# Splitting the gather of a mixture-of-experts layer by halves of the experts

## The reference

```
affinity = softmax(x @ gate_w)                  # 512 tokens x 8 experts, per batch
gating, index = top_k(affinity.T, K=128)        # each expert picks its 128 tokens
x_sel = x[index]                                # 8 experts x 128 tokens x 128
h = silu(x_sel @ Wg[e]) * (x_sel @ Wu[e])       # 128 -> 256
out = (h @ Wd[e]) * gating                      # 256 -> 128
x_out = zeros.at[index].add(out)                # scatter back
```

## Time and profile before

| | before |
|---|---|
| median of three runs | 482.2 us |
| profiled execution, its time | 482.52 us |
| its span, first to last instruction | 480.8 us |
| TensorE busy | 397.7 us, 83% |
| VectorE busy | 385.2 us, 80% |
| ScalarE busy | 232.2 us, 48% |
| GpSimd busy | 54.5 us, 11% |
| mean granted TensorE clock | 0.933 |

### The profile page before, as it was taken

The page is one execution under the profiler, slowest core; times in us unless marked ns, Lnnn a source line. Parts: engine busy times, 40 slices in busy tenths (PEclk is TensorE's granted clock), DMA queues, the critical chain, the costliest instruction groups (busy, mean ns, idle before and its releaser), DMA issues.

```text
span 480.8 us, 7695 instructions
## 1 busy us (share of the span) xinstructions
PE 397.7 (83%) x2204; PEld 213.2 (44%) x2204; DVE 385.2 (80%) x841; ACT 232.2 (48%) x439; POOL 54.5 (11%) x103
## 2 busy tenths in 40 slices
PE   2702999999778889999999999999977019999995
PEld 1600456776543543333333333334427004567764
DVE  6698957788789888999898899987546889577883
ACT  2400453432341157777777777778863003543322
POOL 4520002122000010000000000000014400011210
PEclk9999999999897669999999999999996558999998
DMA  6100002223069721111112111100200000022103
GB/s 178 46 0 0 1 1 67 65 58 92 4 237 287 274 79 46 45 46 46 44 49 56 60 49 52 44 1 2 67 1 0 0 1 1 1 65 65 41 25 89
DMA packets 25767, 27.48 MB, mean 57 GB/s; under 512 B 3920, under 2 KB 17488, under 8 KB 25680
## 3 DMA queue, kind: packets, MB, share of 16 engines
q1 hardware_dynamic: 25744, 27.20, 18.6%
HBM read 17.08 MB, written 9.98 MB: 56 GB/s over the span
## 4 chain that ended last, share of the span: by engine, by line
PE 64%; DVE 16%; issue 12%; ACT 4%; POOL 1%; DMA 1%; DVEq 0%; ACTq 0%; POOLq 0%
PE ps L1151 14%; PE ps L1161 13%; PE ps L1136 6%; PE ps L1038 5%; DVE probs L748 4%; DVE neg_max L810 3%; PE ps L1021 3%; PE ps L1053 3%; PE ps L1023 3%; PE ps L1054 3%; PE ps L1022 3%; ACT probs L599 2%; PE ps L963 2%; PE ps L1170 2%; DVE heads_out L709 2%
## 5 line engine op out<-in xcount | busy, mean ns | idle before, releaser
L810 DVE TENSOR_REDUCE neg_max<-ps 128x1 f32<-128x512 f32 x256 | 161.1, 681 | 14.3 <-PE ps L1136 14.2
L599 ACT ACTIVATE probs<-ps 128x512 f32<-128x512 f32 x256 | 136.8, 601 | 44.0 <-PE ps L1151 42.8
L1136 PE MATMUL ps<-stacks 63*128 63x512 f32 x256 | 105.7, 494 | 3.3 <-DVE neg_max L810 2.6
L1151 PE MATMUL ps<-stacks 64*128 64x512 f32 x256 | 95.0, 462 | 4.9 <-ACT probs L599 4.8
L1151 PEld LDWEIGHTS ps<-stacks 64*128 64x128 f32 x256 | 41.3, 190 | 76.3 <-ACT probs L599 65.7
L1161 PE MATMUL ps<-probs,v_ext 128*32 128x512 f32 x512 | 69.0, 612 | 0.0
L1136 PEld LDWEIGHTS ps<-stacks 63*128 63x128 f32 x256 | 43.8, 196 | 19.5 <-DVE neg_max L810 15.0
L525 ACT CAST stacks<-ps 128x512 fp32r<-128x512 f32 x32 | 17.2, 588 | 67.5 <-PE ps L1002 67.5
L771 DVE TENSOR_TENSOR vae_and_gates<-heads_out,ps 128x512 f32<-128x512 f32 x32 | 21.9, 686 | 21.3 <-ACT heads_out L533 19.3
L453 POOL TENSOR_TENSOR w_lo<-w_gu,w_hi 128x512 fp32r<-128x512 f32 x16 | 20.6, 1295 | 150.1 <-ACT w_hi L512 150.1
L748 DVE TENSOR_TENSOR probs<-slot_row,slot 128x1024 f16<-128x1024 f16 x32 | 36.5, 1219 | 0.1
(11 more groups left out here) (150 smaller groups left out, 539.2 us busy)
## 6 DMA issues: line engine op xcount, KB each, us to landing
stacks<-parts_dram SPq DMA_DIRECT2D x64, 128.0 KB, 2.4
parts_dram<-part_hi SPq DMA_DIRECT2D x8, 512.0 KB, 3.5
parts_dram<-part_lo SPq DMA_DIRECT2D x8, 512.0 KB, 5.8
w_gu<-in_L_ffn_Wg_dram SPq DMA_DIRECT2D x16, 128.0 KB, 2.1
w_gu<-in_L_ffn_Wu_dram SPq DMA_DIRECT2D x16, 128.0 KB, 2.2
wd_sb<-in_L_ffn_Wd_dram SPq DMA_DIRECT2D x16, 128.0 KB, 2.2
x<-in_L_attn_x_dram SPq DMA_DIRECT2D x4, 256.0 KB, 3.7
stacks<-k_rows_dram SPq DMA_DIRECT2D x2, 512.0 KB, 6.6
```

Source lines behind the costliest of these rows:

```text
L599: nc.scalar.activation(probs[:, u // HG, u % HG, :], ps[:, RING + ring_bank(step, u), :], ACT.Exp, scale=SCORE_SCALE).then_inc(probs_ready, 1)
L810: nc.vector.tensor_reduce(neg_max[:, g, col, qt:qt + 1], ps[:, ring_bank(step, u), :], AX.X, ALU.max, negate=True).then_inc(max_taken, 1)
L1136: nc.tensor.matmul(ps[:, ring_bank(step, u), :], q_stack[rows, g, pp, chunk(qt)], k_stack[rows, g, pp, :], start=True, stop=True).then_inc ...
L1151: nc.tensor.matmul(ps[:, RING + ring_bank(step, u), :], k_stack[rows, g, pp, chunk(c)], q_stack[rows, g, pp, :], start=True, stop=True).th ...
```

## The change

The gather is divided by halves of the experts instead of by batches alone.

- VectorE makes the masks of experts 0 to 3 for all four batches first (16 instructions of 512 numbers per partition in place of 1024), and those of experts 4 to 7 in between the work for the first two experts.
- TensorE gathers experts 0 to 3 of all batches, starts `experts` when their 8 copies are done, and gathers the second half in four pieces: gate_up(0), gather, down(0), gather, gate_up(1), gather, gather. The four products of zeros that clear banks 0 to 3, and turn_down(0), come after these.
- ScalarE's copies of the second half, and the rounding of the weights of experts 2 and 3, stand in the new order too; the first turn of ScalarE's loop is written out.
- The facts are reduced in two halves, so that there are four reductions.
- Eight products of zeros into bank 2 (`WARM_UP`) come ahead of the gather.

```
-                for b in range(B):
-                    pe.wait_ge(halves_ready[l], b + 1)
-                    if b == 0:
-                        pe.wait_ge(facts_ready[l], CL)
-                    for hf in range(2):
...
+                for _ in range(WARM_UP):
+                    nc.tensor.matmul(ps[:, 2, :], zeros[:, 0:P], zeros[:], start=True, stop=True)
+                pe.wait_ge(facts_ready[l], CL)
+                for b in range(B):
+                    pe.wait_ge(halves_ready[l], b + 1)
+                    gather(l, b, 0)
+            def gather(l, b, hf):
+                if hf == 0 and b == 3:
+                    pe.wait_ge(picked_ready[l], 2)
+                if hf == 1:
+                    pe.wait_ge(picked_ready[l], 2 * B + 2 * max(b - 1, 0))
+                for c in range(C):
+                    pe.wait_ge(pick_ready[l], B * C * hf + C * b + c + 1)
+                    for bank, half in zip(pick_banks(b, hf), (xn_hi, xn_lo)):
+                        last = nc.tensor.matmul(ps[:, bank, :], half[:, C * b + c, :], pick[:, b, c, EH * hf:EH * hf + EH, :], ...)
+                last.then_inc(gathered[l], 1)
+                if hf == 1 and b == 0:
+                    pe.wait_ge(slot_facts_ready[l], 2)
+                for e in range(EH * hf, EH * hf + EH):
...
             def experts(l):
-                pe.wait_ge(picked_ready[l], 4 * B)
+                pe.wait_ge(picked_ready[l], 2 * B)
...
                 gate_up(0, 0)
-                pe.wait_ge(slot_facts_ready[l], 2)
+                gather(l, 0, 1)
+                down(0, 0)
+                gather(l, 1, 1)
+                gate_up(0, 1)
+                gather(l, 2, 1)
+                gather(l, 3, 1)
+                pe.wait_ge(slot_facts_ready[l], 4)
+                pe.wait_ge(picked_ready[l], 4 * B)
                 for b in range(B):
                     nc.tensor.matmul(ps[:, b, :], zeros[:, 0:P], zeros[:], start=True, stop=True)
-                down(0, 0)
-                gate_up(0, 1)
                 turn_down(0, 0)
```

VectorE's order in `experts` and ScalarE's:

```
+                make_picks(l, 0, 1)
+                read_facts(l, 0)
+                make_picks(l, 1, 1)
                 gate_times_up(0, 0)
                 dve.wait_ge(slot_facts_ready[l], 2)
                 make_place(0, 0)
+                make_picks(l, 2, 1)
                 gate_times_up(0, 1)
+                make_picks(l, 3, 1)
+                read_facts(l, 1)
                 weigh(0, 0, before=False)
...
                 silus(0, 0)
+                copy_picked(l, 0, 1)
+                copy_down(0, 0)
+                copy_picked(l, 1, 1)
+                silus(0, 1)
+                copy_picked(l, 2, 1)
+                copy_picked(l, 3, 1)
+                round_weights(l, 0, 2)
+                copy_down(0, 1)
+                silus(0, 2)
+                round_weights(l, 0, 3)
```

More of the change, by code:

```diff
@@ L275, in after, with pick_banks @@
             return i * (2 * per) + (per * o + more)
-        def pick_bank(n):
-            return 2 + 2 * (n % 3)
+        EH = E // 2
+        WARM_UP = 8
+        def pick_banks(b, hf):
+            if hf == 0:
+                return ((2, 3), (4, 5), (6, 7))[b % 3]
+            return ((2, 3), (0, 7))[b % 2]
         block = ctx.enter_context(nc.Block())
@@ L520, in route, with copy_picked @@
                 round_weights(l, 0, 1)
[L521 to L526, removed]
+                for b in range(B):
+                    copy_picked(l, b, 0)
+            def copy_picked(l, b, hf):
+                act.wait_ge(gathered[l], B * hf + b + 1)
+                for bank, picked in zip(pick_banks(b, hf), (picked_hi, picked_lo)):
+                    nc.scalar.copy(picked[:, EH * hf:EH * hf + EH, b, :],
+                                   ps[:, bank, :].rearrange("p (e s) -> p e s", e=EH)).then_inc(picked_ready[l], 1)
             def experts(l):
@@ L539, in experts @@
                 silus(0, 0)
-                with act.Fori(0, E // 2 - 1) as i:
+                copy_picked(l, 0, 1)
[8 more added lines that the diff above has]
+                round_weights(l, 0, 3)
+                with act.Fori(1, E // 2 - 1) as i:
                     for o in (1, 2):
@@ L746, in route, with make_picks, read_facts @@
                 for b in range(B):
[L747 to L755, removed]
+                    make_picks(l, b, 0)
+            def make_picks(l, b, hf):
+                at, of_slots = slice(EH * hf, EH * hf + EH), slice(b * E + EH * hf, b * E + EH * hf + EH)
+                for c in range(C):
+                    nc.vector.tensor_tensor(pick[:, b, c, at], slot_row[:].unsqueeze(1).broadcast_to([P, EH, K]),
+                                            slot[:, c, of_slots].unsqueeze(2).broadcast_to([P, EH, K]),
+                                            ALU.is_equal).then_inc(pick_ready[l], 1)
+            def read_facts(l, hf):
+                dve.wait_ge(facts_gathered[l], hf + 1)
+                by_slot = ps[:, 1, 0:5 * BE].rearrange("p (b e w) -> p b e w", b=B, w=5)
+                at = slice(EH * hf, EH * hf + EH)
+                nc.vector.tensor_reduce(indexT[:, :, at], by_slot[:, :, at, 0:2], AX.X, ALU.add).then_inc(slot_facts_ready[l], 1)
+                nc.vector.tensor_reduce(gateT[:, :, at], by_slot[:, :, at, 2:5], AX.X, ALU.add).then_inc(slot_facts_ready[l], 1)
             def experts(l):
@@ L990, in route @@
                     pe.wait_ge(rot_ready, 2)
+                for _ in range(WARM_UP):
+                    nc.tensor.matmul(ps[:, 2, :], zeros[:, 0:P], zeros[:], start=True, stop=True)
+                pe.wait_ge(facts_ready[l], CL)
                 for b in range(B):
                     pe.wait_ge(halves_ready[l], b + 1)
-                    if b == 0:
-                        pe.wait_ge(facts_ready[l], CL)
-                    for hf in range(2):
[L996 to L1010, removed]
+                    gather(l, b, 0)
[4 more added lines that the diff above has]
+                    pe.wait_ge(picked_ready[l], 2 * B + 2 * max(b - 1, 0))
+                for c in range(C):
+                    pe.wait_ge(pick_ready[l], B * C * hf + C * b + c + 1)
+                    for bank, half in zip(pick_banks(b, hf), (xn_hi, xn_lo)):
+                        last = nc.tensor.matmul(ps[:, bank, :], half[:, C * b + c, :], pick[:, b, c, EH * hf:EH * hf + EH, :],
+                                                start=(c == 0), stop=(c == C - 1))
+                last.then_inc(gathered[l], 1)
+                if hf == 1 and b == 0:
+                    pe.wait_ge(slot_facts_ready[l], 2)
+                for e in range(EH * hf, EH * hf + EH):
+                    col = 5 * (b * E + e)
+                    for c in range(C):
+                        last = nc.tensor.matmul(ps[:, 1, col:col + 5], pick[:, b, c, e, :], facts[:, c, b, e, :], start=(c == 0), stop=(c == C - 1))
+                if b == B - 1:
+                    last.then_inc(facts_gathered[l], 1)
```

## The result

| | before | after |
|---|---|---|
| median of six runs each | 482.12 us | 479.65 us |
| lowest and highest | 481.94 to 482.81 | 477.55 to 480.02 |
| profiled execution, its time | 482.52 us | 479.99 us |
| its span | 480.8 us | 478.3 us |
| mean granted TensorE clock | 0.933 | 0.930 |

The ratio of the runs is 0.9931, with a 95% interval of 0.9916 to 0.9945: 3.3 us faster by the ratio, 2.5 by the medians and by the spans. The forecast was 480.2 us, 2.0 us faster. The direction and the mechanism held. The sum for the two stages was too small, and it had no term for another stretch, whose length differs from profile to profile.

The account below looks back on a forecast made before the run. Masks were taken to bound the gather and TensorE what follows; stages of 33.22 and 33.62 us become 32.1 plus 0.3 for the clock, gaining 0.8 and 1.2: 482.2 - 2.0 = 480.2 us, range 479.2 to 481.4 (8 in 10: 478.8 to 483.1).

Parts of the forecast that it names:

- The half mask: VectorE's masks in the gather: one of 512 numbers takes 0.600 us; 32 cost 19.2 us against 18.2.
- the start of gate_up(0): First expert's products start 11.5 us behind the first mask, where before it was 21.8: 10.3 us sooner.
- VectorE is in time for down(0): First expert's down products: gate_times_up(0) ends at 16.3 us, down(0) wants it at 16.8, so 0.5 us to spare.
- one new hole: TensorE ahead of the zeros clearing banks 0 to 3: waits for the last gather's copy, some 0.8 us idle.
- the wait for expert 2's weights goes: First stage, third gate_up: GpSimd has the weights split at 31.2 us, against 32.1 when TensorE wants them.
- Rival (a): Expert stages: VectorE becomes the bound, or order switches cost as much; 1.3 to 1.5 us per stage, 482.4 us; chance 0.24.
- Rival (b): Gather: zeros don't bring the clock's rise forward; 0.4 to 2.0 us slower, middle 483.4; chance 0.16.
- the sum of the two stages: Both expert stages: 1.2 us gained in the first and 0.8 in the second, together 2.0 us.
- The clock: Start of the gather: slow products before the clock's rise cost nothing to 0.6 us, taken as 0.3 in either stage.
- TensorE's list: TensorE from gate_up(0) to the third gate_up: expert products, gather pieces, new wait and clearing zeros sum to 20.6 us.
- The yardstick: Each stage measured from first mask to third gate_up's start, 33.62 and 33.22 us before; a shift there shifts the end.
- a shift of the attention's length: Attention part: should shift as a whole; changing its own length was listed as a sign of being wrong, without size.

Follow-up runs that it names:

- before_zeros: Only the eight products of zeros ahead of the gather, added to the kernel before: 482.28 us against 482.63, ratio 0.9982.
- before_tail: Eight products of zeros in TensorE's waits behind the last attention step, added to the kernel before: 481.57 us against 482.26, ratio 0.9975.
- no_zeros: The change without its eight products of zeros ahead of the gather (WARM_UP = 0): 479.73 us, ratio 0.9927 to the kernel before.
- early_clear: The change with banks 2 and 3 cleared ahead of the wait for the last copies and facts: 477.59 us, ratio 0.9893 to the kernel before.
- the block: The change with the gather's second half in one block between gate_up(0) and down(0): 476.47 us, ratio 0.9865 to the kernel before.

## Why the prediction fell short

**What held.** The half mask at 0.602 us (taken 0.600); the start of gate_up(0) at 11.55 us (11.5); that VectorE is in time for down(0); one new hole, ahead of the clearing zeros, 0.87 us (0.8); that the wait for expert 2's weights goes: in the first stage the rounding ended at 73.6 and GpSimd at 74.9, ahead of the third gate_up at 76.4. Rival (a), VectorE as the bound behind the first half, is out by the mask's 0.602 and the chain after; the switches that it priced at 0.24 each cost 0.10 at down(0) (1.82 against 1.72), 0.11 at gate_up(1) (0.34 against 0.23) and 0.02 at a quarter of the gather. Rival (b), zeros that don't bring the clock up, by the run without them.

**The step that failed is the sum of the two stages, and in it three terms were mis-sized**, for the second stage 0.8 forecast and 1.6 measured:
- The clock, taken as 0.3 us in each stage, cost nothing in either profile: the last products of the first half waited for the masks, and gate_up(0) was where the masks put it. My range for it, nothing to 0.6, held this; I chose its middle.
- TensorE's list, 20.6 us, is 425.49 - 405.22 = 20.3: three quarters at 2.12 rather than 2.25 us, since 16 small products between large ones take 0.38 on the chain, not half of 1.07, and down(0) at 1.82 rather than 1.96; and the new wait at 1.24 (421.07 to 422.31) rather than 1.37; gate_up(1) and the clearing zeros took 0.12 and 0.14 more.
- The yardstick. I measured to the start of the third gate_up. Before, it started from a wait in both stages, in the second a short one that the chain does not name: GpSimd's split of its weights ended at 427.55, and the first weights were loaded at 427.70. Its twelve products took 2.99 us on the chain; after, it runs on from down(1) and takes 2.76. This 0.2 us restart lay behind my end point.

```profile
426.28 1.27 POOL L453 TENSOR_TENSOR w_lo<-w_gu,w_hi 128x512 fp32r<-128x512 f32 x1 [47.48 <-ACT w_hi L512]
...
427.70 0.19 PEld L1021 LDWEIGHTS ps<-stacks,w_hi 128*128 128x128 f32 x1 [0.76 <-issue]
```


Together 0.3 + 0.3 + 0.2 make the missing 0.8; in the first stage, 1.2 forecast and 2.1 measured, the same three are 0.3, 0.35 and 0.27.

The 3.7 us of the two stages is also a matter of which profile of before one takes. In the one on record GpSimd's split in the first stage took 1.54 us, in the other two profiles with before's masks and order (before_zeros and before_tail) 1.26, and their turn-down points are 36.05 and 36.04 in the first stage and 35.97 and 35.82 in the second. Against these the change gained 3.2 and 3.0 us in its stages, still more than 2.0.

**What the sum did not have** is the tail. I counted a shift of the third gate_up as a shift of the end. It is, until a stretch with little TensorE work, where the clock fell 7.7 us behind the heads in the profile of before and 1.7 behind them in that of the change: 1.4 us lost in both profiles of the change, nothing in those of no_zeros and early_clear. The stretch was visible before: the earlier trace rows show the clock falling behind the attention, and I named a shift of the attention's length only as something that would prove me wrong, without a price. The profile of before had the short tail, that of after the long one, so the spans, 2.5 us apart, show less than the 3.7 of the stages. Without that difference in the tail they would be 3.9 apart; the ratio's 3.3, over runs whose tails no profile shows, lies between.

The rule of the Trainium skill (TensorE: Matmul & The Clock Gate, "What's actually happening"), that the windows run freely, fits moments of change that differ between profiles, but no run here shows it, and I expected its scatter in the wrong place, at the zeros. There, the rise came at 44.8 to 47.6 us of the first stage in the profiles with zeros, and moved gate_up(0) by 0.1 us at most. More is lost or won elsewhere: the tail runs from 36.6 to 38.4 us over the twelve profiles, and the stretch ahead of it, from the first stage's turn-down point to the heads, from 275.4 to 277.2. The runs of the change scattered 2.5 us against 0.9 before in the first set, but only 1.4, less than before's, in the second, so the wider scatter that I derived from it is not shown.

**Open.** Why the stretch ahead of the tail differs by 1.8 us; why the first stage of the kernel without zeros starts its masks 0.4 us later; why the tail's zeros bring 0.8 us on the change but 0.3 on the block; and whether the tail moves between executions of one kernel, and in what share of them it is long, for which twelve profiles of eleven kernels are few.

## What to carry to other kernels

Before splitting a stage to start its consumer sooner, add up both engines' work in it: where the two sums are close, the early start is only worth the idle time that it removes, and the place to look is the holes that the new order makes (here a clear that needs a bank just copied from; a plain block order without that hole gained another 2 us and more). Measure a shift past the restart of the next stage, not at its first instruction. And where a chain has stretches with little TensorE work, price the clock in them before and after: a few products of zeros in waits that exist anyway held it in the four kernels here that had them.

## What the runs showed of the hardware

- With eight products of zeros ahead of the gather, the clock rose from 1.2 to 2.4 GHz at 44.8 to 47.6 us of the first stage; without them at 49.0 to 51.2.
- The clock fell although TensorE had not stopped: by the windows of before it was busy 1.86 and 2.65 of 4 us at 2.4 GHz ahead of the fall at 365.2. In twelve profiles it fell at 1.6 to 2.2 or at 7.4 us and more behind the same instruction, never between. Between the first two groups of the table that was worth 1.0 to 1.4 us of a 37 us stretch.
- Executions of one kernel differ in their mean granted clock: for the kernel before 0.919 to 0.936 over 50 of them, with about 1.0 us between the average times of the 30 lowest and the 20 highest.
- The window rows of the first stage of before say 1.00 from 46 to 50 us while products there are 0.43 us apart as at 1.2 GHz, so the distances of the products had to be read for the clock ahead of its first rise.
